# Cross phase: attention products put directly behind the next chunk's scores, and ScalarE's copies in another order

## What is computed

```
K, Q, V  = context @ Wk2, x1 @ Wq2, context @ Wv2        # 16 heads of 32
energy   = Q K^T ; lengths = number of nonzero energies of query 0, per head
score    = softmax(energy / sqrt(32), columns past the length cut off)
x2       = layernorm(x1 + score V)
out      = layernorm(x2 + relu(x2 @ fc1^T + b1) @ fc2^T + b2)
```

## Time and profile before

| | |
|---|---|
| median of three runs | 2798.56 us (2794.96 to 2801.65) |
| profiled execution | 2798.25 us, its span 2796.5 us |
| mean granted TensorE clock | 0.991 |
| busy, share of the span | TensorE 97%, its weight loads 85%, VectorE 67%, ScalarE 56%, GpSimd 27% |
| one turn of the cross phase | 51.04 us, 14 such turns |
| chain that ended last, first line | cross_work L172, 15% of the span |

### The profile page before, as it was taken

How to read it: one execution, slowest core, us unless ns; L and a number is a source line. 1 busy time by engine, 2 the same in 40 slices (tenths; PEclk the granted TensorE clock), 3 DMA queues, 4 the chain that set the end, 5 groups by cost and what they waited for, 6 DMA issues and landing times. The chain is left out here.

```text
span 2796.5 us, 68809 instructions
## 1 busy us (share of the span) xinstructions
PE 2716.7 (97%) x24256; PEld 2363.5 (85%) x24256; DVE 1885.6 (67%) x5488; ACT 1562.8 (56%) x4829; POOL 744.2 (27%) x935
## 2 busy tenths in 40 slices
PE   5999999998999999999999999999999999999997
PEld 5888888887888888888888888888888888888886
DVE  5788888876444443435387777777777767777766
ACT  5777777766211111111277777777665666666664
POOL 2332333331000000001023333333233324324333
PEclk9999999999999999999999999999999999999999
DMA  4323333341311211113031111113011111101100
GB/s 149 102 97 106 109 122 100 99 140 69 106 37 54 60 45 45 44 46 103 18 92 45 45 45 45 45 45 110 32 46 38 38 45 45 45 31 45 45 30 24
DMA packets 148214, 180.54 MB, mean 65 GB/s; under 512 B 16432, under 2 KB 77872, under 8 KB 147632
## 3 DMA queue, kind: packets, MB, share of 16 engines
q1 hardware_dynamic: 148144, 179.63, 20.1%
HBM read 122.97 MB, written 56.62 MB: 64 GB/s over the span
## 5 line engine op out<-in xcount | busy, mean ns | idle before, releaser
L2743 ACT ACTIVATE mlp_h<-mlp_f,mlp_b1col 128x512 f32<-128x512 f32 x128 | 88.2, 690 | 529.9 <-PE mlp_f L2948 529.9
L2948 PE MATMUL mlp_f<-mlp_xT_hi,mlp_w 128*128 128x512 f32 x1024 | 337.0, 391 | 4.2 <-issue 4.2
L2966 PE MATMUL mlp_acc<-mlp_w,mlp_hT_hi 128*128 128x512 f32 x1024 | 315.3, 389 | 2.1 <-DVE mlp_hT_lo L2851 2.1
L2849 DVE CAST mlp_hT_hi<-mlp_h 128x512 fp32r<-128x512 f32 x128 | 57.7, 450 | 376.7 <-ACT mlp_h L2743 376.5
L817 ACT ACTIVATE mask_prob<-mask_scores,mask_low 128x256 f32<-128x256 f32 x512 | 237.6, 485 | 106.4 <-DVE mask_low L1339 106.4
L817 ACT ACTIVATE cross_prob<-cross_scores,cross_low 128x256 f32<-128x256 f32 x512 | 237.5, 499 | 8.0 <-DVE cross_low L1333 7.9
L1339 DVE CUSTOM_DVE_ANT_0 mask_scores<-mask_scores,mask_mask 128x256 f32<-128x256 f32 x512 | 198.9, 461 | 54.6 <-PE mask_scores L1942 54.3
L2948 PEld LDWEIGHTS mlp_f<-mlp_xT_hi,mlp_w 128*128 128x128 f32 x1024 | 193.3, 189 | 45.1 <-issue 5.0
L2966 PEld LDWEIGHTS mlp_acc<-mlp_w,mlp_hT_hi 128*128 128x128 f32 x1024 | 192.2, 188 | 42.2 <-DVE mlp_hT_lo L2851 2.5
L172 PE MATMUL causal_work<-causal_xT_hi,causal_w 128*128 128x256 f32 x1008 | 227.3, 296 | 0.2
L817 ACT ACTIVATE causal_prob<-causal_scores,causal_low 128x128 f32<-128x128 f32 (+1 forms) x512 | 211.3, 436 | 19.2 <-DVE causal_low L1339 17.9
(11 more groups left out here) (343 smaller groups left out, 8277.2 us busy)
## 6 DMA issues: line engine op xcount, KB each, us to landing
cross_x_in<-after_attention SPq DMA_DIRECT2D x17, 512.0 KB, 3.7
mask_x_in<-in_x SPq DMA_DIRECT2D x16, 512.0 KB, 4.6
mask_c_in<-in_ctx SPq DMA_DIRECT2D x16, 512.0 KB, 5.4
mask_res<-in_x SPq DMA_DIRECT2D x16, 512.0 KB, 3.7
after_attention<-mask_res SPq DMA_DIRECT2D x16, 512.0 KB, 2.8
mlp_x<-after_attention SPq DMA_DIRECT2D x8, 1024.0 KB, 5.6
mlp_stage<-in_L_xattn_fc_w SPq DMA_DIRECT2D x8, 1024.0 KB, 5.6
after_layer<-mlp_y SPq DMA_DIRECT2D x8, 1024.0 KB, 4.3
```

What stands on the lines that cost most here:

```text
L2743: act.activation(h32[:, m % 2, :], F1[m % 2][:], ACT.Gelu, bias=b1col[:, m:m + 1]).then_inc(s["gelu"], 1)
L2849: dve.tensor_copy(hT[0][:, r, :], h32[:, r, :]).then_inc(s["h_hi"], 1)
L2948: ins = pe.matmul(F1[m % 2][:], W[2 * (m // 4)][:, a, k, m % 4 * P:(m % 4 + 1) * P], xT[p][:, k, :], start=(k == 0 and n == 0), stop=(k == ...
L2966: ins = pe.matmul(ACC[t][:], hT[a][:, m % 2, t * P:(t + 1) * P], W[2 * (m // 4) + 1][:, p, m % 4, :], start=(m == 0 and n == 0), stop=(m = ...
```

## The change

TensorE's queue: at the start of a turn and for chunks 0 and 2, `attend` of one chunk now follows at once on `scores` of the next; the transposes of the fourth head go ahead of the scores, and `queries` behind `attend`. `feed1(b, 1)` is split in two halves around the transposes of `attended(b, 1)`; the transposes of head 10 go ahead of it. At the turn's end `keys(b + 1, 1)` goes behind the transposes of head 14. ScalarE's queue: copy 2 ahead of the V copy, copy 5 behind the two xT copies, copy 10 ahead of `attended(b, 1)`, copy 11 (where there is a previous element) ahead of the second relu, copy 14 ahead of `qk(b + 1, 1)`. VectorE, GpSimd and SyncE keep theirs. No instruction is added or taken away. `if i == 1` in `feed1` lets the halves be called apart.

```diff
@@ -1063,8 +1063,8 @@
                 qk(b, 2)
                 copy(b, 0)
                 copy(b, 1)
+                copy(b, 2)
                 values(b, 0)
-                copy(b, 2)
 
                 copy(b, 3)
                 for u in (4, 5, 6):
@@ -1077,13 +1077,13 @@
                 copy(b, 4)
                 if not prev:
                     matrix_hi(3, (0, 1))
-                copy(b, 5)
             if nxt:
                 turned(b + 1, 0)
                 turned(b + 1, 1)
             if not prev:
                 matrix_hi(3, (2,))
             if cur:
+                copy(b, 5)
                 copy(b, 6)
                 if not prev:
                     matrix_hi(3, (3,))
@@ -1105,16 +1105,18 @@
                 turned(b + 1, 3)
             if cur:
                 copy(b, 9)
+                copy(b, 10)
                 attended(b, 1)
+                if prev:
+                    copy(b, 11)
             if prev:
                 relu(b, 1)
             else:
                 matrix_hi(4, (0,))
             if cur:
-                copy(b, 10)
                 if not prev:
                     matrix_hi(4, (1,))
-                copy(b, 11)
+                    copy(b, 11)
                 for u in (12, 13, 14):
                     exps(b, u)
                 attended(b, 2)
@@ -1126,10 +1128,10 @@
                 copy(b, 13)
             if not prev:
                 matrix_hi(4, (2, 3))
+            if cur:
+                copy(b, 14)
             if nxt:
                 qk(b + 1, 1)
-            if cur:
-                copy(b, 14)
 
         def turn(b, prev, cur, nxt):
             if cross:
@@ -2021,7 +2023,7 @@
                 m = 2 * p + i
                 ins = product(pe, (W0 if p else W1)[:, i * S:(i + 1) * S],
                               lambda k, a: W[3][:, a, k, m * P:(m + 1) * P], lambda k, q: x2T[q][:, k, :])
-            if i:
+            if i == 1:
                 ins.then_inc(s["f1_ps"], 1)
 
         def feed2(b, t):
@@ -2325,17 +2327,12 @@
 
         def cross_turn(b, prev, cur, nxt):
 
-            if cur and prev:
+            if prev:
+                turn_probs(b, -1)
                 scores(b, 0)
-            if prev:
-                turn_probs(b, -1)
-            if cur and prev:
+                attend(b, -1)
                 pe.wait_ge(s["qk_lo"], KC * b + 2)
                 queries(b, 2)
-
-            if prev:
-                attend(b, -1)
-            if cur and prev:
                 keys(b, 2)
                 turn_probs(b, 0)
 
@@ -2348,20 +2345,18 @@
                 attended(b, -1)
 
             if cur:
-                values(b, 0, 1)
                 pe.wait_ge(s["len_ready"], KC * b + 2)
                 turn_probs(b, 2)
+                values(b, 0, 1)
+                turn_probs(b, 3)
 
             if cur:
                 scores(b, 1)
-                turn_probs(b, 3)
-                pe.wait_ge(s["qk_lo"], KC * b + 3)
-                queries(b, 3)
-
-            if cur:
                 if not prev:
                     pe.wait_ge(last["z_done"], KC * B + 1)
                 attend(b, 0)
+                pe.wait_ge(s["qk_lo"], KC * b + 3)
+                queries(b, 3)
                 keys(b, 3)
                 turn_probs(b, 4)
 
@@ -2421,35 +2416,29 @@
 
             if cur:
                 attend(b, 1)
-            if prev:
-                if cur:
-                    pe.wait_ge(s["v_ready"], 2 * b + 2)
-                else:
-                    pe.wait_ge(s["proj_read"], TT * (b - 1) + 1)
-                feed1(b, 1)
-            else:
-                pe.wait_ge(s["v_ready"], 2 * b + 2)
-                shift_through(1)
-            if cur:
-                attended(b, 1)
                 pe.wait_ge(s["len_ready"], KC * b + 4)
                 turn_probs(b, 10)
-
-            if cur:
+            pe.wait_ge(s["v_ready"], 2 * b + 2)
+            if prev:
+                feed1(b, 1, (0,))
+                attended(b, 1)
+                feed1(b, 1, (1,))
+            else:
+                shift_through(1)
+                attended(b, 1)
+
+            if cur:
+                turn_probs(b, 11)
                 if nxt:
                     pe.wait_ge(s["t_lo"], NP * (b + 2))
                 scores(b, 3)
-                turn_probs(b, 11)
+                attend(b, 2)
             if nxt:
                 if prev:
                     pe.wait_ge(s["f1_act"], 2 * (b - 1) + 1)
                 else:
                     pe.wait_ge(s["bias_done"], 1)
                 queries(b + 1, 0)
-
-            if cur:
-                attend(b, 2)
-            if nxt:
                 keys(b + 1, 0)
             if cur:
                 turn_probs(b, 12)
@@ -2471,12 +2460,13 @@
                 pe.wait_ge(s["proj_read"], TT * (b - 1) + 2)
                 feed2(b, 1)
             if nxt:
-                keys(b + 1, 1)
                 pe.wait_ge(s["len_ready"], KC * (b + 1) + 1)
             elif cur:
                 turned_free(b, 3)
             if cur:
                 turn_probs(b, 14)
+            if nxt:
+                keys(b + 1, 1)
 
         def turn(b, prev, cur, nxt):
             if cross and not cur:
```

More of the change, by code:

```diff
@@ L2326, in cross_turn @@
         def cross_turn(b, prev, cur, nxt):
-            if cur and prev:
-                scores(b, 0)
             if prev:
                 turn_probs(b, -1)
-            if cur and prev:
+                scores(b, 0)
+                attend(b, -1)
                 pe.wait_ge(s["qk_lo"], KC * b + 2)
                 queries(b, 2)
-            if prev:
-                attend(b, -1)
-            if cur and prev:
                 keys(b, 2)
```

## The result

The changed kernel takes 2807.7 us, the median of 7 runs (2806.16 to 2809.32), against 2798.56 for the kernel before, also 7 runs (2794.96 to 2804.07): a ratio of 1.0031, 95% interval 1.0021 to 1.0040. It is slower by 9.1 us. The profiled execution of the changed kernel took 2807.75 us with a span of 2806.1, against 2798.25 and 2796.5 before. The lines of the code have moved by two: L1924 of before is L1926 here, L1942 is L1944, L1963 is L1965.

The account below looks back on a forecast made before the run. TensorE, busy 50.73 of 51.04 us, was taken as the bound. Per turn +0.61 for late q0 minus 0.06 saved gives +0.55, +7.7 over 14 turns; +0.5 for turns 0 and 15 makes +8.2: 2806.5 us, range 2797 to 2815.

Parts of the forecast that it names:

- F: End of `feed1(b, 1)` on TensorE: 2.97 us after `attend(b, 1)` ends before the change, forecast 3.67 after it.
- wait for q0: TensorE at `energies0(b+1, 0)` would wait 0.71 us for GpSimd's q0, where before the chain was hidden.
- turns 0 and 15: First and last cross turns: each counted as at most one turn like the others, together +0.5 us.
- The switches: TensorE's changes between kinds of matmul: scores to `attend` no dearer than scores to transposes; 0.58 us saved before displaced transposes.
- the copies: ScalarE copies for heads 3, 15, 11 just before `attend`: priced at nothing, covered by scores; otherwise 0.1 to 0.3 us per merge.
- The saving ahead of scores(b, 2): First two merges: 0.06 us saved per turn before `scores(b, 2)`, bounds 0 and 0.4, because VectorE's xT_lo arrives together with TensorE.
- the chain's head: Start of VectorE's chain to xT_lo: placed on GpSimd, whose row work on y holds a VectorE multiply for 0.92 us.
- The relu behind copy 11: ScalarE after feed1(b, 1): relu 1 waits for transposes it does not need, delaying the chain to q0 by 0.94 us.
- faster: Rival: no new wait at `energies0` if q0 is ready by F + 9.42; 0.4 us a turn kept, 2792 us; chance 0.09.
- Cancelling: Rival: 0.2 to 0.4 us saved before `scores(b, 2)`, taken back at `energies0`; +0.1 to +0.35 a turn, 2800 to 2804; chance 0.27.
- The port: Rival: VectorE's instruction on y precedes GpSimd's second half of q0, blocking it 0.75 us; +1.46 a turn, 2819 us; chance 0.07.

Follow-up runs that it names:

- relu first: The changed kernel with ScalarE's second relu ahead of copy 11 again, TensorE's new order kept: 2796.11 us, ratio to before 0.9993.
- two merges alone: The changed kernel with chunk 2 as before on TensorE and ScalarE; merges at the turn's start and of chunk 0 stay: 2797.06 us, ratio 0.9995.
- the kernel without the shift: The changed kernel without GpSimd's addition of the last norm's shift on y, cross phase, all but the last batch element: 2803.41 us, ratio to before 1.0015.
- the third merge alone: The kernel before with only chunk 2 and the split feed1 as in the changed kernel, on TensorE and ScalarE: 2809.35 us, ratio 1.0040.
- ScalarE's order on the kernel before: The kernel before with ScalarE taking copies 10 and 11 ahead of the second relu, TensorE's order untouched: 2829.54 us, ratio 1.0113.
- the last version: The kernel with relu first and `attended(b, 0)` later, plus head 8's transposes moved ahead of feed1(b, 0) on TensorE: 2788.07 us, ratio to before 0.9965.
- relu first and `attended(b, 0)` later: The changed kernel with relu ahead of copy 11, and ScalarE's copy of attended(b, 0) behind exponential 7 and chunk 3's Q/K copy: 2793.02 us, ratio to before 0.9983.
- The four kernels with relu first: The changed kernel with relu ahead of copy 11: alone 2796.11 us; Q/K copy before exponential 7, 2795.87; attended(b, 0) later, 2793.02; that plus head 8's transposes moved, 2788.07.

## Why the prediction was right

Forecast was 2806.5 us, range 2797 to 2815, slower; measured 2807.7. Step by step, for the turn shown above:

| step | predicted | measured |
|---|---|---|
| scores to `attend` | 1.15 | 1.14 and 1.16 |
| `attend` to the product behind it | 1.00 | 1.00 |
| end of `attend(b, 1)` to F | 3.67 | 3.56 |
| copy 11, relu 1 | F + 0.64, F + 1.14 | F + 0.64, F + 1.13 |
| minima, first exponential | F + 3.07, F + 3.82 | F + 3.07, F + 3.79 |
| TensorE free for `energies0` | F + 9.42 | F + 9.43 (relu first, no wait) |
| `energies0` starts | F + 10.13 | F + 10.11 |
| wait for q0 | 0.71 | 0.68 |
| saved ahead of `scores(b, 2)`, mean of 12 turns | 0.06 | 0.02 (two merges alone: 0.04) |
| a turn | +0.55 | +0.46 |
| turns 1 to 14 | +7.7 | +6.5 |
| turns 0 and 15 together | +0.5 | +4.4, of it 2.8 the clock |

The rows that the prediction names add up to q0 at F + 10.11 and not F + 10.13 (3.82 + 3.94 + 0.69 + 0.89 + 0.72 + 0.05), so its own sum was +0.53 a turn and +7.4 over 14; the forecast moves by 0.3 us.

**The switches and the copies.** Both as priced: a switch from scores to `attend` is not dearer than one to transposes, and no `attend` of turns 1 to 14 waits for a copy in the changed kernel.

**The saving ahead of scores(b, 2).** That it would be lost to VectorE is shown by the two merges alone: turn 50.97, a saving of 0.06. The reason was only half right. The prediction had the chain's head on GpSimd; the kernel without the shift shows that GpSimd's work does hold the multiply, by 0.9 us, and that the scores hold the minima just as long. The merges themselves did this: with the transposes of heads 15 and 3 ahead of the scores, `scores(b, 1)` starts 17.45 us behind `energies0(b, 0)`, where it was 17.13, and the minima of chunk 1 start at 18.73, where they were at 18.62 (means of 12 turns). A shorter queue of TensorE as a whole is thus a later one at that place. From the minima to `scores(b, 2)` 0.13 is won back. The Trainium skill (SBUF — State Buffer, section Who interferes with whom) says that a VectorE instruction with two SBUF inputs and a GpSimd one that reads SBUF exclude each other; 1.08 against 0.17 us agrees, for the addition on y. GpSimd's small q0 operations ran beside the same multiply and did not hold it, so here the rule did not show with every pair. Only an earlier GpSimd and earlier scores together would give room, which no kernel here tried.

**The relu behind copy 11.** Shown by its own experiment: with relu first the wait of 0.7 is gone and the turn is 50.80. This also measures the rival "faster": where its condition holds, as it does with relu first, a turn changes by -0.23 and not by -0.42, since 0.22 of TensorE's saving goes into the wait for xT_lo. In the changed kernel its condition, q0 ready by F + 9.42, failed: q0 was ready at F + 10.05.

**The mis-sized terms.** A turn was forecast 0.09 too long; the stretch with the split `feed1` alone was 0.11 too long (3.56 for 3.67). Turns 0 and 15 were counted as one more turn at most, and cost 4.4. In turn 15 the step that the prediction named is there: its transposes of head 12 wait 2.10 us for the exponential,

```profile
2763.03 0.66 PE L1965 MATMUL cross_scores<-all_ident,cross_prob 128*128 128x128 f32 x4 [2.10 <-ACT cross_prob L817]
```

where the kernel before has no wait there, and the kernels with relu first wait 1.18. In the last turn nothing of the next batch element stands in front of these transposes, so the same lateness has no cover. But the wait alone is not that stretch's +2.35. TensorE comes to it sooner than before, by its shorter queue and because the transposes of head 15 are already done at the cut, and so these transposes start only 0.50 later behind `scores(15, 0)` (37.23 for 36.73). The larger part stands behind the wait: the granted clock fell to 0.50 there, where the changed kernel without the shift, with the same wait of 2.10, kept 1.00, and that is 1.59 us (last section). The other 0.26 are spread over the end. Turn 0 is +2.01: 1.20 is the lower granted clock behind a wait that both kernels have (last section), 0.33 is the order of the work, in it the wait for q0 that went from 1.95 to 2.12, and 0.46 only moved over the cut: the transposes of head 15 now stand ahead of `scores(1, 0)`, as in every turn, where `energies0` to the next `scores` went from 6.58 to 7.04. So the work that the change brought outside turns 1 to 14 is 1.6 us where 0.5 was forecast, and the clock, which the forecast did not count, is 2.8. That the two totals agree to 1.2 us is thus partly luck: -1.2 in the turns, +3.9 in the first and the last, and -1.25 ahead of the cross phase, where nothing of the work differs.

**The rivals.** Cancelling did not happen: the turn is +0.46, above the +0.35 that it allowed. The port did not turn round: GpSimd's second half of q0 was done at 2358.19, and VectorE's instruction on y had started at 2358.03, when that half was already running. Neither was lengthened, with 0.72 and 0.75 us as in the earlier trace rows, so what a turned order would have cost no run shows.

## What to carry to other kernels

Shortening the engine that sets the end is worth only what the others are early by: before moving work on it, write down for each of its waits how long before need its data is ready, and recompute that for the new order. In an in-order queue, an instruction that waits for late data must not stand ahead of one whose data is there and on which a long chain hangs; here that exchange cost 0.70 us a turn, and undoing it is one line. Work moved ahead of a product makes all that hangs on the product later, also where it saves time for the engine as a whole. When one wait is removed, look for what stood just behind it (scores behind GpSimd, the exponential behind the Q/K copy), and count the first and last iteration by themselves, since their cover differs, and a wait that is long there can bring the lower clock with it.

## What the runs showed of the hardware

In turn 0 TensorE waits twice for about 2 us: for the second xT_lo ahead of `scores(0, 2)`, and for q0 at `energies0`. Neither wait is new, but the clock behind them is not the same in each trace. The first wait, before and after, and the busy times of the ten microseconds from 1976 (columns as above):

```profile
1976.76 0.63 PE L1942 MATMUL cross_scores<-cross_qk_parts 32*128 32x256 f32 x12 [2.17 <-DVE cross_xT_lo L1290]
```

```profile
1976.00:1986.00 10.00, 7.47 (x82) 6.66 (x83) 7.99 (x16) 6.00 (x22) 5.89 (x5) 1.00 0.14 54
```

```profile
1975.53 0.87 PE L1944 MATMUL cross_scores<-cross_qk_parts 32*128 32x256 f32 x12 [2.18 <-DVE cross_xT_lo L1292]
```

```profile
1976.00:1986.00 10.00, 9.22 (x79) 8.63 (x75) 6.75 (x13) 5.86 (x21) 4.61 (x4) 0.67 0.15 54
```

The same wait, to 0.01 us; before, the clock stays at 1.00, after, it goes to 0.50, the lower of the two levels (1.2 of 2.4 GHz), and TensorE is busier with fewer matmuls. The wait is in nine of the eleven traces, 1.77 to 2.19 long, and the clock fell behind it in four: the changed kernel, the third merge alone, ScalarE's order on the kernel before, and the last version. From this wait's end to the next `energies0(1, 0)` are 21.93 us before, 23.46 in the changed kernel and 22.26 with relu first, whose queue on TensorE is the changed kernel's and whose clock stayed up: 1.20 us for the lower clock, 0.33 for the order of the work.

Behind the second wait, 1.94 to 2.12 long, the clock fell in ten of eleven traces. Here the kernel before, the changed one, and the version with relu first and `attended(b, 0)` later, the one that kept it:

```profile
1999.00:2001.00 2.00, 2.00 (x16) 2.00 (x15) 1.58 (x7) 0.00 (x0) 0.00 (x0) 0.78 0.00 0
```

```profile
1999.00:2001.00 2.00, 2.00 (x12) 2.00 (x13) 1.28 (x6) 0.29 (x1) 0.00 (x0) 0.66 0.00 0
```

```profile
1999.00:2001.00 2.00, 2.00 (x19) 2.00 (x18) 1.53 (x5) 0.60 (x1) 0.00 (x0) 1.00 0.00 0
```

From `energies0` to the next scores that version took 4.30 us. The changed kernel, with the same order of TensorE's work there, took 5.82: 1.5 us for the lower clock.

A third such wait came with the change, the one of 2.10 in turn 15. The clock fell behind it in the changed kernel and with the third merge alone, and stayed up in the kernel without the shift. From the end of the wait to the next short wait, the same 23 matmuls, in the changed kernel and then without the shift:

```profile
2763.03:2768.93 5.90, 5.66 (x23) 4.46 (x23) 1.40 (x4) 3.75 (x15) 0.00 (x0) 0.71 0.00 0
```

```profile
2761.20 0.66 PE L1968 MATMUL cross_scores<-all_ident,cross_prob 128*128 128x128 f32 x4 [2.10 <-ACT cross_prob L820]
```

```profile
2761.20:2765.51 4.31, 4.08 (x23) 3.29 (x23) 1.41 (x4) 3.74 (x15) 0.00 (x0) 1.00 0.00 0
```

The four kernels with relu first wait 1.18 at this place, and all kept 1.00. So a wait of some 2 us on an engine that was otherwise full can cost another 1.2 to 1.6 us behind it, and whether it does is not set by its length alone. In a comparison of a few microseconds that is a scatter to look for first. The waits of 0.7 in turns 1 to 14 did not bring it in the turn shown, which ran at 1.00.
